# Turning the graph branch back to rows with a true f32 matmul instead of a transpose

## What is computed

```python
xn = layernorm(x)
# graph branch: h = xn @ W, summed over 100000 edges and the own node, both ends scaled
out = segment_sum(h[src] * norm, dst) + conv_bias
y = (out - mean(out)) / (std(out) + EPS) * ln_weight + ln_bias
gnn = where(y >= 0, y, prelu_a * y)
x1 = x + gnn + attention(xn)
# experts: the best two of eight for every row
logits = (layernorm(layernorm(x1)) * gamma + beta) @ Wr + br
result = x1 + sum over the two of weight * (gelu(. @ W1[e] + b1[e]) @ W2[e] + b2[e])
```

## Time and profile before

| | us |
|---|---|
| median of three runs | 1380.14 |
| lowest and highest run | 1376.36, 1380.92 |
| the profiled execution, its own time | 1381.24 |
| its span, first to last instruction | 1379.4 |
| TensorE (PE) busy | 1246.9 |
| VectorE (DVE) busy | 937.7 |
| GpSimd (POOL) busy | 812.9 |
| ScalarE (ACT) busy | 540.4 |

### The profile page before, as it was taken

One profiled execution on the slowest core, in us unless ns is written; L12 is line 12 of the kernel. 1 busy time (PEld: TensorE's weight loads), 2 busy tenths in 40 slices (PEclk: granted clock), 3 DMA queues, 4 the chain that ended last, 5 costly groups with the idle time before them and its releaser, 6 DMA issues. The chain is left out here.

```text
span 1379.4 us, 30236 instructions
## 1 busy us (share of the span) xinstructions
PE 1246.9 (90%) x8165; PEld 1100.0 (80%) x8166; DVE 937.7 (68%) x2880; ACT 540.4 (39%) x1420; POOL 812.9 (59%) x785
## 2 busy tenths in 40 slices
PE   4997688999899999999998796985799999999998
PEld 4984687887789888887787545983699999999997
DVE  8998787787888778778883267678444444444444
ACT  7707301222233333333311102436455555555553
POOL 1294677777777777777777100001376666666665
PEclk9999898999999999999999796555799999999999
DMA  7005333335666666688998501358344444444443
GB/s 244 0 0 183 110 107 105 104 104 170 193 194 204 196 200 206 208 242 277 276 293 259 194 0 43 110 174 278 83 73 69 67 70 70 72 69 69 71 69 41
DMA packets 138726, 189.66 MB, mean 137 GB/s; under 512 B 22229, under 2 KB 116924, under 8 KB 138372
## 3 DMA queue, kind: packets, MB, share of 16 engines
q0 software_dynamic: 43440, 90.29, 28.3%
q1 hardware_dynamic: 95188, 98.24, 22.4%
HBM read 155.97 MB, written 33.44 MB: 137 GB/s over the span
## 5 line engine op out<-in xcount | busy, mean ns | idle before, releaser
L759 POOL DMA_INDIRECT RG<-table,srci x484 | 474.5, 980 | 153.9 <-issue 150.4
L776 PEld LDWEIGHTS ps<-S_t,RG 128*128 128x128 f32 x1936 | 259.5, 197 | 31.5 <-DMA RG<-table,srci 20.9
L776 PE MATMUL ps<-S_t,RG 128*128 128x96 f32 x1936 | 265.1, 279 | 16.0 <-DMA RG<-table,srci 15.6
L799 PE MATMUL ps<-zrow,R 128*128 128x256 f32 (+1 forms) x784 | 221.3, 390 | 18.6 <-DMA zrow<-table 12.1
L2029 POOL DMA_INDIRECT out<-R,S_t x105 | 166.3, 1583 | 99.8 <-DVE R L1999 60.0
L1912 PE MATMUL ps<-R,RG 128*128 128x128 f32 x1680 | 207.4, 278 | 0.0
L1912 PEld LDWEIGHTS ps<-R,RG 128*128 128x128 f32 x1680 | 198.4, 194 | 0.2 <-issue 0.2
L1922 PE MATMUL ps<-R 128*128 x840 | 198.6, 380 | 0.0
L1036 DVE TENSOR_TENSOR R<-R,ps 128x245 f32 (+4 forms) x300 | 142.1, 474 | 69.4 <-PE ps L787 46.5
L1945 ACT ACTIVATE R<-ps,RG 128x128 f32<-128x128 f32 x420 | 119.7, 367 | 176.2 <-PE ps L1912 176.2
L1995 DVE TENSOR_TENSOR R<-ps,R 128x256 f32<-128x256 f32 x105 | 44.6, 425 | 202.6 <-PE ps L1922 202.6
(11 more groups left out here) (363 smaller groups left out, 1956.1 us busy)
## 6 DMA issues: line engine op xcount, KB each, us to landing
zrow<-table SPq DMA_DIRECT2D x384, 128.0 KB
RG<-table,srci POOLq DMA_INDIRECT x484, 3.3
ntable<-R SPq DMA_DIRECT2D x12, 516.0 KB, 7.5
table<-RG SPq DMA_DIRECT2D x12, 512.0 KB, 2.9
out<-R SPq DMA_DIRECT2D x12, 512.0 KB, 2.9
R<-in_x SPq DMA_DIRECT2D x6, 896.0 KB, 6.7
R<-in_w SPq DMA_DIRECT2D x8, 514.0 KB, 7.4
slot<-in_x SPq DMA_DIRECT2D x32, 128.0 KB
```

Source lines behind the costliest of these rows:

```text
L759: nc.gpsimd.indirect_dma_start(out=grows[:, s, :], out_offset=None, in_=table, in_offset=bass.IndirectOffsetOnAxis(ap=srci[:, ND + q, c:c ...
L776: last = nc.tensor.matmul(window(q % 2)[:, h, :], grows[:, s, h * P:(h + 1) * P], S_t[:, q % 2, c, :], start=c == 0, stop=c == GC - 1)
L799: nc.tensor.matmul(psD[:, 0:D], adj[b % 2][0:n, j, :], zrow[0:n, i % ZR, :], start=j == 0, stop=j == T - 1).then_inc(z_used, 1)
```

## The change

In `back`, each of the two transposes of a 128x128 f32 block becomes a matmul with the same block as the stationary operand and the identity as the moving one. It writes the same values to the same place. Nothing else is changed: the waits, the semaphores, the order of the instructions on each engine and their number in the program are as before (each such instruction of the program may be executed as several of the array).

```diff
                     for k in range(KC):
-                        last = nc.tensor.transpose(psW[t % 2][:, k * P:(k + 1) * P], acc[:, k, t * P:(t + 1) * P],
-                                                   ident[:, :])
+                        last = nc.tensor.matmul(psW[t % 2][:, k * P:(k + 1) * P], acc[:, k, t * P:(t + 1) * P],
+                                                ident[:, :], start=True, stop=True)
                     last.then_inc(px_ok, 1)
```

## The result

The kernel became faster: 1359.86 us (median of four runs, 1358.59 to 1363.61) against 1379.43 us for the kernel before beside it, a ratio of 0.9865 (95% interval 0.9839 to 0.9892). The gain is small, 1.35%, but clear of the noise. It is 19.6 us less, where 21 us more were forecast. It is what the first rival describes: the clock rises in the loop.

A forecast was written before the change was run, and what follows sets the result against it. The prediction took TensorE at half clock in the residual loop as the bound. It added 21.7 us for 49 tiles, less 0.8 for a wait at the start: +21 on 1380.14, 1401 us, range 1395 to 1405.

The forecast's parts named there:

- the first rival: Residual loop: the clock rises to full there, making it 14 to 21 us faster, 1363 us; chance 0.16.
- What bounds the kernel: Residual loop: TensorE sets the pace at granted clock 0.50; the loop's loss or gain moves the kernel's end equally.
- The price at the low clock: `back` in the loop: two more instructions of 0.221 us, a tile going from 1.60 to 2.04 us.
- The term of +0.44 us a tile: `back` in the loop: the added time of two more instructions, 21.7 us for 49 tiles.
- the upper bound of 0.46: `back` in the loop: at most 0.46 us more a tile, +22.5 us over 49 tiles.
- the fourfold price: `back` in the loop: true matmuls cost four times the transposes, +65 us, 1445 us; chance 0.01.
- the clock staying low: Residual loop: the granted clock stays 0.50 throughout, giving +21 us, 1395 to 1405 us; chance 0.80.
- The rival's own sum: Loop if the clock rises: 7 us at the old clock, then 45 tiles of 1.11 to 1.26: 57 to 64 us.
- The no-cost rival: `back` in the loop: L1505 keeps its rate, as identity recognised or second instruction hidden: 1380 us; chance 0.03.

The follow-up runs named there:

- kernel with late matmuls: Kernel before, with `back` as true matmuls from tile 6 on, transposes in tiles 0 to 5: 1402.0 and 1402.1 us; five more runs, 1363.2 to 1403.0 us.
- both bursts: Kernel before plus unused work ahead of the residual loop: 16 f32 matmuls, 1353.7 us, or 32 f32 transposes, 1352.45 us.
- the new order: Kernel before with `logits` issued seven steps behind in place of three, and six `turned` slots in place of two: 1348.17 to 1353.61 us, ratio 0.9786.
- the doubled transposes: Kernel before with every transpose of `back` issued twice to the same place: median 1358.44 us, ratio 0.9839.

## Why the prediction was wrong

**What bounds the kernel** was right: TensorE at half clock. When the clock rose, the loop shrank and the end moved by as much; everything behind it only shifted.

**The price at the low clock** was somewhat too small. The kernel with late matmuls had it in isolation: +20.1 us in the medians and +22.4 in the traces of the loop, with 43 of the 49 tiles changed, against 19 expected. A tile measured 2.13 us and not 2.04, since a true matmul instruction took 0.248 us among transposes and 8-column matmuls and not the 0.221 of line 1912. The term of +0.44 us a tile is thus 0.53, and the upper bound of 0.46 was too low; for 49 tiles, an estimate, it would have been about +25 us. The price is still about twofold, since `back` went from 0.46 to 0.99 us. The fourfold one of the Trainium skill (page "TensorE: Matmul & The Clock Gate", section "Terms") is refuted for this shape.

**The step that failed** is the path on which all of the forecast's +21 us rests, "the clock staying low", to which I gave 0.80. The clock rose 4.3 us after the first `back`. The error lies in the weighing of the first rival, "In the changed loop 0.88 us of each 2.04 is such work ... That is nearer to the stretches that stayed low". It has three faults, and the runs show each:

- It judged the loop by a steady tile. The loop's start is another program: three `back` steps with nothing between. The runs with matmuls up to tile 5 or tile 2 have the whole gain from there, and the list of steps quoted ahead of the prediction shows it to anyone who writes out s = 0, 1, 2.
- It asked which work would lift the clock and never which would hold it. These differ: the very mixture that stayed at 0.50 for 75 us stays at 1.00 once it begins there, in five different kernels (first six tiles, first three, both bursts, the new order).
- It took it from a sentence of the Trainium skill (the same page, section "Part 4: PE-mode transpose") that transposes don't count, and wrote that the trace agrees. The trace had transposes together with 8-column matmuls, so it couldn't tell the kinds apart. The burst of transposes, the doubled transposes and the new order did. With `flip` counted too, the changed tile has 1.31 us of 128-column work in its 2.04 (0.88 + 0.43), and not 0.88.

**The rival's own sum** was good: 14 to 21 us less, 1363 us, against 19.6 less and 1359.86 measured. Its sizes were a little off. The time at the old clock was 4.3 us (850.07 to about 854.4) and not 7. TensorE needs 1.11 us a tile and not 1.02, mostly since the cold tile is 2.13 and not 2.04; its parts about halve alike, `back` from 0.99 to 0.52, `flip` from 0.43 to 0.22 and `logits` from 0.71 to 0.37 us. VectorE, expected as the bound, has 41.45 us of 44.00, so both are nearly full, and it becomes the bound only where the extra instructions go. The chance of 0.16 looks too low, though one result can't show it: where the rows had f32 instructions of 96 or 128 columns in a row, the clock had risen.

**The no-cost rival and the fourfold price** didn't occur: L1505 has 196 instructions.

## What to carry to other kernels

Where TensorE is busy all the time at half clock, look at what runs in the first microseconds of the stage, not at its steady tile: a start of 128-column instructions alone may lift the clock for a whole stage whose own work holds it but doesn't lift it. Here it came from the order of the work, by letting the small matmuls join four steps later, for four more buffers; a burst into idle time did the same. Time such a kernel several times, since near the border a single run misleads. Before a slower instruction is put in for its effect on the clock, use it in the first tiles only.

## What was not expected of the hardware

- The granted clock depends on its history: the old loop, with PE busy for 50.00 of 50.00 us, ran at 0.50. Behind a burst it ran at 1.00, with PE busy for only 38.28 of 45.00 us.
- A busy share doesn't tell whether the clock will rise: it rose after a start with PE busy for 4.89 of 7.00 us, all 128-column instructions, and stayed low after one with 5.52 of 7.00, among them 8-column ones.
- Transposes lift the clock as matmuls do: 32 of them in 6.03 us did.
- The same program can come out up to 40 us apart, by whether its clock rises in a stage: 1363.2 to 1403.0 us in five runs of one kernel, where 0.50 in the loop is shown for a run of 1400.3.
